# Attention's projection and output jobs over 44 of 48 ticks instead of 36

## The reference

```python
c_q, c_kv = x @ W_DQ, x @ W_DKV              # latents of 64
Q = concat(c_q @ W_UQ, rope(c_q @ W_QR))     # 16 heads of 16 + 8
K = concat(c_kv @ W_UK, rope(x @ W_KR))      # the rope part is shared by the heads
scores = where(causal, clip(Q @ K.T, -80, 80), -inf)
attn = softmax(scores / sqrt(24)) @ (c_kv @ W_UV)
x = x + layernorm(attn_of(layernorm(x)) @ W_O)
```

## Time and profile before

| | |
|---|---|
| median of three runs | 2999.1 us |
| the profiled execution | 3002.68 us, of which the span is 3001.0 |
| mean granted clock of TensorE | 0.929 of full |
| TensorE (PE) busy | 2602.1 us (87%) |
| DVE busy | 2386.0 us (80%) |
| ACT busy | 1868.1 us (62%) |
| POOL busy | 642.7 us (21%) |
| first scores of the first batch | 81.25 us from the start of the span |
| one steady batch of attention | 133.15 us (464.05 to 597.20) |
| last scores begin | 1098.6 us |

### The profile page before, as it was taken

How to read it: one execution, slowest core, us unless ns; L and a number is a source line. 1 busy time by engine, 2 the same in 40 slices (tenths; PEclk the granted TensorE clock), 3 DMA queues, 4 the chain that set the end, 5 groups by cost and what they waited for, 6 DMA issues and landing times. The chain is left out here.

```text
span 3001.0 us, 42994 instructions
## 1 busy us (share of the span) xinstructions
PE 2602.1 (87%) x16008; PEld 1808.0 (60%) x16008; DVE 2386.0 (80%) x4031; ACT 1868.1 (62%) x2947; POOL 642.7 (21%) x441
## 2 busy tenths in 40 slices
PE   3888888888888971799999999999999999997986
PEld 2233333333333321688888888888888888886875
DVE  4577777767777664879888999889889898876998
ACT  1676766767676750666666766667666676664332
POOL 2013121111202010211212112121121221112666
PEclk8798989989998985999999999999999999998998
DMA  3451525435251503000000000000000000003231
GB/s 103 82 86 60 85 82 90 82 72 89 64 89 53 89 29 89 1 1 15 15 15 1 15 15 15 15 1 15 15 15 15 1 15 8 8 8 117 85 105 56
DMA packets 125681, 136.28 MB, mean 45 GB/s; under 512 B 17394, under 2 KB 105714, under 8 KB 125476
## 3 DMA queue, kind: packets, MB, share of 16 engines
q1 hardware_dynamic: 125476, 133.54, 19.3%
HBM read 87.10 MB, written 46.40 MB: 44 GB/s over the span
## 5 line engine op out<-in xcount | busy, mean ns | idle before, releaser
L385 ACT ACTIVATE probs<-psum_a 128x1024 f32<-128x1024 f32 (+3 forms) x768 | 601.0, 816 | 317.6 <-PE psum_a L654 313.6
L1418 PE MATMUL psum_f<-w,picked 128*128 128x256 f32 (+1 forms) x2304 | 721.6, 346 | 0.0
L1417 PE MATMUL psum_f<-w,picked 128*128 128x256 f32 x2304 | 620.5, 286 | 1.2 <-DVE picked L1240 1.2
L1418 PEld LDWEIGHTS psum_f<-w,picked 128*128 128x128 f32 x2304 | 445.8, 193 | 56.3
L461 DVE TENSOR_SCALAR probs<-probs 128x2048 f32<-128x2048 f32 (+3 forms) x320 | 303.8, 949 | 184.3 <-ACT probs L385 184.2
L1417 PEld LDWEIGHTS psum_f<-w,picked 128*128 128x128 f32 x2304 | 446.6, 194 | 1.5 <-DVE picked L1240 1.5
L654 PE MATMUL psum_a<-q_stack,k_stack 72*128 72x512 f16 (+3 forms) x1536 | 393.9, 347 | 38.1 <-ACT probs L385 17.6
L669 PE MATMUL psum_a<-probs,v 128*17 128x512 f32 (+3 forms) x3072 | 341.3, 518 | 1.8 <-DVE probs L461 1.7
L1049 ACT ACTIVATE gates<-psum_f 128x256 f32<-128x256 f32 (+1 forms) x384 | 185.9, 486 | 239.0 <-PE psum_f L1418 237.3
L1240 DVE TENSOR_TENSOR picked<-hid,masks 128x512 fp32r<-128x512 f32 x512 | 322.9, 690 | 14.2 <-PE psum_f L1418 11.2
L654 PEld LDWEIGHTS psum_a<-q_stack,k_stack 72*128 72x128 f16 x1536 | 99.8, 100 | 381.4 <-ACT probs L385 217.9
(11 more groups left out here) (282 smaller groups left out, 5558.0 us busy)
## 6 DMA issues: line engine op xcount, KB each, us to landing
heads_scratch<-kq_parts SPq DMA_DIRECT2D x64, 256.0 KB
k_stack<-heads_scratch SPq DMA_DIRECT2D x96, 128.0 KB
q_stack<-heads_scratch SPq DMA_DIRECT2D x96, 128.0 KB
x_in<-x_dram SPq DMA_DIRECT2D x8, 1024.0 KB, 5.4
x_res<-x_dram SPq DMA_DIRECT2D x16, 512.0 KB, 4.8
x_scratch<-y SPq DMA_DIRECT2D x16, 512.0 KB, 3.1
xs<-x_scratch SPq DMA_DIRECT2D x16, 512.0 KB, 3.8
xf_scratch<-xs SPq DMA_DIRECT2D x16, 512.0 KB, 2.9
```

Source lines behind the costliest of these rows:

```text
L385: act.activation(probs[:, s % PROB_SETS, 2 * u:2 * u + 2, q0:512], psum[:, 2 * u:2 * u + 2, q0:512], ACT.Exp, scale=exp_scale).then_inc(ex ...
L1417: pe.matmul(soft_out, x, cols[:, 1], start=start, stop=stop)
L1418: return pe.matmul(gate_out, x, cols[:, 2] if it == 0 else cols[:, 0::2], start=start, stop=stop)
```

## The change

The two tables place the same 32 jobs in the same order but for one pair: OR(1,0) and OR(1,1), which stood between the projections of the first half, now stand between LAT(1,0) and QR(1,0). A steady window uses 32 of the ticks 0 to 43, mostly two ticks with a job and one without. Statistics and normalisation of y follow their jobs (first tick 9 in place of 8, and 34 in place of 20), `x_moments` comes in tick 38 in place of 37, and POOL's queue has k_rope and q_rope of the second half ahead of `add_residual` of the second half. No instruction is added or taken away, and no wait.

```diff
-    PROJECTION = {3: ("XT", 0, 0), 4: ("XT", 0, 1), 7: ("KR", 0, 0), 8: ("LAT", 0, 0), 11: ("QR", 0, 0), 12: ("QR", 0, 1),
...
-                  30: ("KH", 1, 0), 31: ("KH", 1, 1), 32: ("QH", 1, 0), 33: ("QH", 1, 1), 34: ("V", 1, 0), 35: ("V", 1, 1)}
...
-              9: ("OT", 1, 0), 10: ("OT", 1, 1), 17: ("OR", 1, 0), 18: ("OR", 1, 1)}
+    PROJECTION = {3: ("XT", 0, 0), 4: ("XT", 0, 1), 8: ("KR", 0, 0), 9: ("LAT", 0, 0), 14: ("QR", 0, 0), 15: ("QR", 0, 1),
...
+                  36: ("KH", 1, 0), 37: ("KH", 1, 1), 39: ("QH", 1, 0), 40: ("QH", 1, 1), 42: ("V", 1, 0), 43: ("V", 1, 1)}
...
+              11: ("OT", 1, 0), 12: ("OT", 1, 1), 31: ("OR", 1, 0), 32: ("OR", 1, 1)}
...
                 if 0 <= after < BATCH:
                     q_rope(after, 0)
+                if 0 <= after < BATCH:
+                    k_rope(after, 1)
                 if 0 <= before:
                     y_scale(before, 1)
+                if 0 <= after < BATCH:
+                    q_rope(after, 1)
+                if 0 <= before:
                     add_residual(before, 1)
-                if 0 <= after < BATCH:
-                    k_rope(after, 1)
-                    q_rope(after, 1)
                 if 0 <= after + 1 < BATCH:
                     x_scale(after + 1)
...
-                    for half, first in ((0, 8), (1, 20)):
+                    for half, first in ((0, 9), (1, 34)):
...
-                    if t == 37:
+                    if t == 38:
                         x_moments(w + 2)
```

More of the change, by code:

```diff
@@ L62, in last_tick @@
         return (gci // ACCS) * STEPS + last_step[gci % ACCS]
-    PROJECTION = {3: ("XT", 0, 0), 4: ("XT", 0, 1), 7: ("KR", 0, 0), 8: ("LAT", 0, 0), 11: ("QR", 0, 0), 12: ("QR", 0, 1),
[3 rows of a table removed]
-    OUTPUT = {1: ("OT", 0, 0), 2: ("OT", 0, 1), 5: ("OR", 0, 0), 6: ("OR", 0, 1),
-              9: ("OT", 1, 0), 10: ("OT", 1, 1), 17: ("OR", 1, 0), 18: ("OR", 1, 1)}
+    PROJECTION = {3: ("XT", 0, 0), 4: ("XT", 0, 1), 8: ("KR", 0, 0), 9: ("LAT", 0, 0), 14: ("QR", 0, 0), 15: ("QR", 0, 1),
[3 rows of a table added]
+    OUTPUT = {0: ("OT", 0, 0), 1: ("OT", 0, 1), 6: ("OR", 0, 0), 7: ("OR", 0, 1),
+              11: ("OT", 1, 0), 12: ("OT", 1, 1), 31: ("OR", 1, 0), 32: ("OR", 1, 1)}
     job_at = {}
```

## The result

The changed kernel took 3024.2 us (median of six runs, 3013.3 to 3031.5) against 2998.5 us of the kernel before beside it (2994.3 to 3000.3). The ratio is 1.0083 with a 95% interval of 1.0059 to 1.0106: 26 us slower, where 28 us faster was forecast. The profiled execution took 3027.7 us, its span 3026.0. The first scores come at 82.4 us (81.25 before).

What follows compares the result with a forecast made beforehand. TensorE was taken to bound attention, with waits on DVE and low clock added. Legs of 82.9, 28.8 and 16.6 us gave a 128.3 us period against 133.15; with the other pieces -28 us, so 2971 us, range 2926 to 3022.

Steps and rivals of the forecast that it cites:

- What bounds the kernel: Attention stage: TensorE bounds ticks without jobs, 22.14 us a group, 88.6 a batch; 32 jobs cost 44.6 us more.
- the job's price: Attention stage: 0.66 us for each of 32 jobs, from 21.1 us left after waits (15.7) and low clock (7.8).
- leg one: Batch's first score to tick 33: 82.9 us, with waits on DVE cut from 15.7 to 2.0 us.
- Leg two: Tick 33 to DVE's read of QH(1,1): 28.8 us, through DVE's own work and POOL's add_residual and x_scale.
- Leg three: DVE's read of QH(1,1) to the next batch's first score: 16.6 us, mostly the stack load's 13.7.
- The clock: Batch start, behind idle TensorE: low granted clock costs 3.0 us a batch, counted in leg one.
- The boundary wait: Ahead of each batch: TensorE idle, waiting for the stack DMA, about 10 to 12 us.
- The rule of the Trainium skill: DVE instructions with two SBUF inputs are shut out while GpSimd reads SBUF; x_moments would stand, period 129.2 against 128.3 us.
- C: Slower: POOL's chain is longer, QH(1,1) read over 4.8 us later; period 136.1, total 3023 us; chance 0.23.
- B: Tail not late: TensorE's pace sets the read of QH(1,1); period 121.6, total 2931 us; chance 0.14.
- D: No change: the new wait takes just what the old ones gave; total 2999 us; chance 0.15.
- the signs: Profile after: job waits under 5 us, stack wait some 10, x_rstd after add_residual, load 3 us after last read.

Runs made afterwards that it cites:

- y0_late: Changed kernel with the first half's y_normalize in tick 25 instead of 13 and its add_residual behind q_rope of the same half; 2976.7 us, ratio 0.9924.
- warm: `both` plus seven idle fp32 matmuls ahead of TensorE's wait for the stacks at every batch start but the first; 2951.0 us, ratio 0.983.
- dense_front: `both` with the jobs of ticks 0 to 21 back in the ticks of the kernel before; 3044.9 us, ratio 1.0135.
- before_no_add: Kernel before, without POOL's addition of x to the normalised rows (output lacks that residual); 2953.3 us, ratio 0.9823.
- both: Changed kernel with x_scale ahead of the second half's add_residual, first y_normalize in tick 25, its addition behind q_rope; 2971.8 us, ratio 0.9904.
- after_warm: Changed kernel plus seven idle matmuls ahead of TensorE's wait for the stacks; 3013.5 us, ratio 1.0048.
- add0_late: Changed kernel with only the first half's add_residual held back, behind q_rope, until V(0,1) is read; y_normalize stays in tick 13; 3002.8 us, ratio 1.0002.

## Why the prediction was wrong

**What bounds the kernel, and the job's price.** Right, with a slip. Groups with spaced jobs, no long wait and the full clock take 26.1 us with 8 jobs (y0_late), 29.9 with 9 (the changed kernel) and 29.4 with 9 (warm) over a base of 22.14, so 0.50, 0.86 and 0.81 us a job, 0.73 on the mean, around the 0.66 assumed. The 0.66 came from three low stretches where there were four; with the fourth it would have been 0.61, and leg one 1.3 us less. dense_front shows that waits of 1.5 to 1.7 us come from job n - 2 only two ticks back.

**Leg two, tick 33 to the last QH read: 28.8 us.** Measured 28.5, and near in each part: 17.0 us to the end of y_normalize (17.5 forecast), 5.0 from there to x_normalize (5.8), 6.4 for the rest (5.5). TensorE's first scores of tick 33 begin at 566.77, and DVE's read ends at 594.56 + 0.68:

```profile
566.77 0.50 PE L657 MATMUL psum_a<-q_stack,k_stack 72*128 72x384 f16 x2
...
594.56 0.68 DVE L512 TENSOR_TENSOR kq_parts<-psum_a,kq_parts 128x512 f16<-128x512 f32 x1
...
598.09 1.26 SPq L226 DMA_DIRECT2D k_stack<-heads_scratch  x3
...
612.95 1.03 PE L657 MATMUL psum_a<-q_stack,k_stack 72*128 72x512 f16 x2 [6.42 <-DMA q_stack<-q_rope_scratch]
```

**Leg three, the DMAs: 16.6 us.** Measured 17.7 (2.85 for the scratch, 14.9 for the load). Over the batches it is 16.5 to 18.8.

**Leg one, first score to tick 33: 82.9 us. This step failed**: 566.77 - 476.6 = 90.2 us, and 90.2 to 92.9 us over the steady batches. The term was "I take the 15.7 us down to 2 us", with bounds of 0 and 5, and "The clock stretches inside go too". The waits were read as the work of the jobs' spacing alone. Part of them, and of the low clock, is DVE held up by y_normalize and by POOL's add_residual, whatever lies between the jobs: before_no_add shows 53 us of it in the kernel before. With jobs two in three that hold-up falls on one read, OT(1,1), in ticks 13 and 14. It costs 4.2 us of wait and 3.4 to 17.1 us of low clock behind it, which the sum had at nothing. In leg two the prediction had priced the very same thing, from the row of a caught clip, and left it out in leg one. Where y_normalize and its addition are moved off the reads (y0_late), leg one is near the forecast: 83.2 to 85.9 us. In the fourth batch the first groups are alike (34.0 us in both); the second takes 26.1 us in place of 31.8. That y0_late's total, 2976.7 us, lies near the 2971 forecast is in part luck, since a job cost 0.73 us and not 0.66.

**The clock, 3.0 us a batch.** For the stretch that it was meant for, the right size. Behind the seven boundary waits TensorE ran 4.4 to 12.6 us at the lower level, 12.4 in the fourth batch. Taking that away gave 21 us in `both` (warm), 3.0 a boundary, and 11 us in the changed kernel. In the fourth batch alone it is worth 4.6 us (first group 34.0 against 29.4 in after_warm), so of the 7.3 us by which leg one was too long there, 1.6 are this term and 5.7 the second group (31.8 against 26.1). What the sum lacked is the low clock behind the wait before QR(0,1), and a third stretch of 10.2 us in the tail, with the wait before QH(1,1); the latter lies in leg two, which held, so it shows no price of its own.

**The boundary wait.** Forecast 10 to 12 us of idle TensorE, measured 6.4 (4.3 to 8.2 over the seven). The rest stood earlier, as the 4.1 us before QH(1,1): TensorE waited in two places for the one DVE chain, first for the read of KH(1,1) at 587.54, then for what follows the read of QH(1,1) at 594.56.

**POOL and DVE.** The rule of the Trainium skill (SBUF — State Buffer, section "SBUF: two separate sides") was weighed at +0.9 us a batch. What the trace shows in the changed kernel, x_moments beside the second add_residual:

```profile
584.10 2.23 DVE L447 TENSOR_SCALAR x_mean<-moments 128x8 f32<-128x8 f32 x1
...
583.96 2.34 POOL L311 TENSOR_TENSOR y<-y,x_res 128x1024 f32<-128x1024 f32 x1 [1.26 <-DVE y L551]
586.75 2.03 POOL L316 TENSOR_TENSOR x_rstd<-x_veps,half_neg 128x8 f32<-128x8 f32 x1 [0.45 <-DVE x_veps L450]
```

An instruction of 0.17 us took 2.23 and ended with POOL's, 586.33 against 586.30, and x_scale did begin only 0.45 us behind the addition's end. So x_moments stood still as forecast by the rule, though the instruction held here has one input in SBUF and not two, a case that the prediction's wording of the rule does not cover. It cost little in the sum because add_residual was shorter here, 2.34 us, than the 3.56 us of the earlier trace rows.

**The rivals.** The total is C's, 3023 us, which had 0.23. That the two agree to 1 us is luck. C's mechanism was half right: an engine idle ahead of each batch, and a low clock behind it. But it put most of the extra time behind tick 33, where the sum held; the time was lost before it. B did not happen: x_normalize began at 588.82, right behind x_scale's end at 588.78. D's balance is what one gets with half of the hold-up in ticks 13 to 15 gone: add0_late took 3002.8 us, the kernel before 3004.2 in the same runs. Of the signs, x_rstd behind add_residual and the load 3 us behind the read came true; the waits on DVE stayed at 10.4 us, where under 5 were forecast.

**What stays open.** Without the addition on either side the change costs 22 us, and without the low clock at the boundary 11 us less than it did. The two overlap. No run splits the loss of 26 us between the later tail and the normalisation among the reads, because y_normalize was not moved in the kernel before. Nor does one separate the wait before QH(1,1) from the wait for the stacks, since both hang on the one chain in DVE's queue. Whether y_normalize of the second half could be moved off the tail in the same manner was not tried.

## What to carry to other kernels

A wait that is read as "the producer is two places too near" has to be taken apart first: what stood on the waited-for engine in that time, and would it still stand there? Here the same removal (the addition on POOL) run in the kernel before would have shown it. And where work is spread to fill a schedule, the operand that the next round waits for sets how far: spread what nothing hangs on, and give any long block on a shared in-order queue a place in which nobody needs that queue's next reads; moving one normalisation by twelve ticks, with the addition behind it, gave 48 us, where moving 32 jobs had lost 26.

## What the runs showed of the hardware

- Most DVE instructions in SBUF that began while POOL ran an addition of 128x1024 were held until it ended or up to 1.1 us longer, however small they were: 128x8 elements took 2.23 us for 0.17, a normalise pair 2.76 for 0.73, a clip 2.83 for 0.69. Alone an addition took 2.34 us; where it took 3.0 to 5.7, the DVE instructions of its first part kept their time and the last one was held. Beside POOL's rope products a clip took 1.76 us for 0.69. DVE's reads of PSUM beside either kept their 0.68 us, and clips beside POOL's small y_rstd and x_rstd (128x4 and 128x8, 1.4 to 2.1 us) kept their time. Taking the 16 additions away gave 49 us in the changed kernel, where they took 42.2 us in all, and 53 us in the kernel before, where they took 58.7.
- TensorE ran at 1.2 GHz for 4.4 to 12.6 us behind waits of 4.3 to 8.2 us, though it was busy throughout, and the longest wait did not bring the longest stretch: 12.4 us behind 4.3, 4.4 behind 7.6. Seven idle fp32 matmuls inside the wait kept 2.4 GHz behind five of seven waits and gave 21 us.
- The twelve DMAs of one stack load (each into 16 or 8 partitions, for four heads) take 13.7 to 15.9 us from the first issue to the scores, and 1.5 us of it come from the loads queued behind them.
